# Spreading the routing scatters over the tiles and moving the rope's sum on GpSimd, in a two-layer block on one core

## The reference

```python
x = x + _L0_xattn_ref(_layernorm(x), ctx_2048, ids, ...)   # latent attention, 16 heads of 128 + rope part of 64
x = x + _L0_ffn_ref(_layernorm(x), ...)                    # 16 experts, the best 6 per token
x = x + _L1_xattn_ref(_layernorm(x), ctx_2048, mask)       # attention over 128 memory tokens
x = x + _L1_ffn_ref(_layernorm(x), ...)                    # gated MLP of 2048 plus 8 product-key experts per token
```

## Time and profile before

| | us |
|---|---|
| median of three runs | 2090.32 |
| the profiled execution | 2089.45 |
| its span | 2087.7 |
| PE busy in the span | 1836.0 (88%) |
| DVE / ACT / POOL busy | 1205.9 / 870.9 / 822.2 |
| 96 scatters, POOL line 2114 | 99.2 |

### The profile page before, as it was taken

How to read it: one execution, slowest core, us unless ns; L and a number is a source line. 1 busy time by engine, 2 the same in 40 slices (tenths; PEclk the granted TensorE clock), 3 DMA queues, 4 the chain that set the end, 5 groups by cost and what they waited for, 6 DMA issues and landing times.

```text
span 2087.7 us, 39748 instructions
## 1 busy us (share of the span) xinstructions
PE 1836.0 (88%) x13025; PEld 1086.0 (52%) x13029; DVE 1205.9 (58%) x2650; ACT 870.9 (42%) x1790; POOL 822.2 (39%) x691
## 2 busy tenths in 40 slices
PE   1586998998989489999999999997569989999998
PEld 1335666666655256666666666664444434444443
DVE  7854777777766433333333333332785677777776
ACT  3435877777666134334444344442232222212211
POOL 3102336555565533444344444442001344554542
PEclk7698999999999789999999999999689999999999
DMA  5314557776765256666676676453210345565554
GB/s 195 111 61 125 165 177 170 176 181 186 157 148 127 54 168 163 142 141 163 142 166 142 145 170 124 94 87 60 92 45 12 114 143 186 169 210 202 189 181 164
DMA packets 149136, 294.82 MB, mean 141 GB/s; under 512 B 40432, under 2 KB 77936, under 8 KB 144688
## 3 DMA queue, kind: packets, MB, share of 16 engines
q1 hardware_dynamic: 97968, 157.48, 26.5%
q0 software_dynamic: 46368, 126.29, 24.8%
q10 hardware_dynamic: 4608, 8.52, 1.3%
HBM read 426.00 MB, written 78.33 MB: 242 GB/s over the span
## 4 chain that ended last, share of the span: by engine, by line
PE 66%; issue 8%; POOL 8%; DVE 8%; ACT 5%; DMA 4%; another core or an unknown queue 1%; ACTq 0%; SPq 0%; POOLq 0%; DVEq 0%
PE bank L205 19%; PE bank L207 19%; PE bank L206 19%; POOL expert_tokens L2114 3%; PE bank L999 2%; DMA x_sum<-x,work_arena 2%; DVE work_arena L1466 2%; PE bank L1026 2%; ACT xt_arena L1246 1%; POOL work_arena L2091 1%; DVE work_arena L168 1%; DVE ln_st L155 1%; POOL xt_arena L2100 1%; DMA x<-token_rows,work_arena 1%; POOL xt_arena L2110 1%
## 5 line engine op out<-in xcount | busy, mean ns | idle before, releaser
L205 PE MATMUL bank<-work_arena,xt_arena 128*128 (+1 forms) x1285 | 417.9, 327 | 6.9 <-DVE xt_arena L174 3.3
L206 PE MATMUL bank<-work_arena,xt_arena 128*128 (+1 forms) x1285 | 417.7, 327 | 0.0
L207 PE MATMUL bank<-work_arena,xt_arena 128*128 (+1 forms) x1285 | 417.7, 327 | 0.0
L2187 POOL DMA_INDIRECT x_sum<-x,work_arena x111 | 176.3, 1589 | 400.3 <-DMA x_sum<-x,work_arena 176.7
L205 PE MATMUL bank<-work_arena 128*128 128x512 f16 (+1 forms) x680 | 260.7, 386 | 48.5 <-DVE work_arena L1466 20.0
L1940 DVE TENSOR_TENSOR xt_arena<-xt_arena,bank 128x352 f32<-128x352 f32 x111 | 57.8, 521 | 372.4 <-PE bank L207 347.7
L206 PE MATMUL bank<-work_arena 128*128 128x512 f16 (+1 forms) x680 | 261.1, 386 | 0.0
L207 PE MATMUL bank<-work_arena 128*128 128x512 f16 (+1 forms) x680 | 260.4, 385 | 0.0
L205 PE MATMUL bank<-xt_arena,work_arena 128*128 128x512 f16 (+1 forms) x560 | 212.7, 380 | 1.0 <-DVE xt_arena L174 1.0
L206 PE MATMUL bank<-xt_arena,work_arena 128*128 128x512 f16 (+1 forms) x560 | 212.3, 379 | 0.0
L207 PE MATMUL bank<-xt_arena,work_arena 128*128 128x512 f16 (+1 forms) x560 | 212.2, 379 | 0.0
(11 more groups left out here) (254 smaller groups left out, 3823.1 us busy)
## 6 DMA issues: line engine op xcount, KB each, us to landing
work_arena<-expert_w SPq DMA_DIRECT2D x111, 1408.0 KB
work_arena<-expert_w SPq DMA_DIRECT2D x111, 768.0 KB
work_arena<-in_moe_w SPq DMA_DIRECT2D x64, 352.0 KB
expert_w<-work_arena SPq DMA_DIRECT2D x86, 176.0 KB
work_arena<-in_moe_w SPq DMA_DIRECT2D x48, 256.0 KB
work_arena<-in_mlp_w SPq DMA_DIRECT2D x8, 1536.0 KB
work_arena<-in_head_w SPq DMA_DIRECT2D x16, 512.0 KB, 3.5
expert_w<-work_arena SPq DMA_DIRECT2D x64, 128.0 KB
```

What stands on the lines that cost most here:

```text
L205: pe.matmul(o, a_hi, b_hi, start=start, stop=False)
L206: pe.matmul(o, a_hi, b_lo, start=False, stop=False)
L207: return pe.matmul(o, a_lo, b_hi, start=False, stop=stop)
L2187: pool.indirect_dma_start(out=xacc[:, :], out_offset=bass.IndirectOffsetOnAxis(ap=rid[:, i:i + 1], axis=0), in_=ysb[:, b % YB, :], in_offs ...
```

## The change

Only POOL's list changes, in two places. In the second step of a tile (g = 1) the rope's sum now stands in front of the rows' low half. And the 12 scatters of a batch stand three each in steps ready+4, +5, +8 and +9 (g = 3, 0, 3, 0); for the sixth batch, in +4, +5, +6 and +7 (steps 59 to 62). In step 62 there are then six scatters, with three of the seventh batch, which stays where it was.

```diff
+            def places_of(m):
+
+                late = (4, 5, 8, 9)
+                ends = (4, 5, 6, 7)
+                return [(k, q) for q in range(INNER - 2) for k in range(4)
+                        if m == ready(q) + (late if q < INNER - 3 else ends)[k]]
+
...
                 if row_tile(m, 0) is not None:
                     row_rstd(row_tile(m, 0))
-                if row_tile(m, 1) is not None:
-                    row_low(row_tile(m, 1))
                 if t + 1 < NT:
                     if g in (1, 2):
                         rope_sum_pool(t + 1, g - 1)
                     if g in (2, 3):
                         rope_low_pool(t + 1, g - 2)
-                for k in range(3):
-                    if m - 4 - k in SCORES_AT and BATCHES[SCORES_AT[m - 4 - k]][1] == 2:
-                        place_batch(SCORES_AT[m - 4 - k], 4 * k, 4 * k + 4)
+                if row_tile(m, 1) is not None:
+                    row_low(row_tile(m, 1))
+                for k, q in places_of(m):
+                    place_batch(q, 3 * k, 3 * k + 3)
```

## The result

The changed kernel took 2081.72 us (median of six, 2077.45 to 2083.06), the one before 2093.19 (median of six, 2089.49 to 2100.2): ratio 0.9941, interval 0.9922 to 0.9961. It is 0.6% faster, and not the 1.3% forecast: 2063 was too low, and 2081.7 lies outside 2050 to 2079. Two repeats gave 0.9919 (0.9898 to 0.994) and 0.9929 (0.9909 to 0.995).

A forecast was written before the change was run, and what follows sets the result against it. PE holds 66% of the chain, so GpSimd matters only where PE waits for it. Stall -21.1, sum -7.5 and tail +1.5 gave -27.1 against 2089.45, forecast 2063 us; own range 2055 to 2072, 8 in 10 2050 to 2079.

The forecast's parts named there:

- Scatters out of g = 1: Attention tiles with four scatters in g = 1: all five PE waits at line 2096 vanish, gaining 21.1 us, bounds 10.3 to 25.1.
- The 4.0 kept for those: Fifth long tile: PE's "issue" waits at lines 858 and 859, 2.2 + 1.8 us, were expected to stay.
- Scatters in g = 3 and 0 of every tile: POOL in the attention tiles: PE's cover, 6.1 us of slack, hides these scatters; cost 0, bounds 0 and 3.8 us a step.
- The sum ahead of the rows' low half: Second step of a tile: earlier sum gains 11.1 us through ACT, DVE's delay costs 3.6; net gain 7.5.
- The sum by that rule: Sum edit with DVE's full 1.2 us block paid in each of six rank tiles: 11.1 - 7.2 = 3.9 us gained.
- The tail: Last normalizations, steps 61 and 62: six scatters make the third normalization 2.5 us late; 1.5 us lost, bounds 0 and 2.5.
- line 930 at 9.5, just under the 10 set: Sign of being wrong: PE waits at line 930, the ranks, for more than 10 us.
- the clock at 0.95 in tiles that had no stall: Sign of being wrong: a granted clock below 1.00 in tiles without a stall.
- The five long tiles near 30 us: Sign of being right: the five tiles with scatters in g = 1 fall to near 30 us, at clock 1.00.
- the half stall: Rival at line 846: half the stall stays as a new wait, -12 us, 2078; chance 0.13.
- no matter: Rival: order doesn't matter, or tail and next stage's start return the gain; within 10 us of before, 2085; chance 0.06.
- The slower one: Rival: new scatters in g = 3 delay a normalization PE waits for at line 887; +42 less 27, 2105; chance 0.05.

The follow-up runs named there:

- e6b: Changed kernel without the 72 scatters of the first six batches, run again; 2053.73 us, ratio 0.9881 to the kernel before.
- e8b: Changed kernel with two powers of one column and a drain between them on POOL in place of each of the 72 scatters; 2059.88 us, ratio 0.9861.
- e9: Changed kernel without the 72 scatters and with the rope's sum behind the rows' low half, as before; 2055.2 us, ratio 0.9891.
- e8: Changed kernel with one power of one column on POOL in place of each of the 72 scatters, nothing transferred; 2056.23 us, ratio 0.9887.
- e1: Changed kernel with the old order, rows' low half in front of the rope's sum, scatters in their new places; 2067.6 us, ratio 0.994.
- e1b: Repeat of e1 in another set, on the chip of the first; 2084.4 us, ratio 0.9957 to the kernel before.
- e10: Changed kernel without the 72 scatters, with DVE's split behind the heads' split in steps g = 1; 2047.66 us, ratio 0.9848.
- e2: Kernel before with only the new order, rope's sum in front of the rows' low half, scatters in their old places; 2089.26 us, ratio 1.0026.
- e3: Changed kernel with the old order in the six tiles with ranks and the new order elsewhere; 2066.69 us, ratio 0.9937.
- e4: Changed kernel with DVE's weight split of a tile's second step behind the heads' low half; 2065.68 us, ratio 0.9921.
- e6: Changed kernel without the 72 scatters of the first six batches; one execution, 2055.22 us, beside 2078.17 for the changed kernel.
- e4b: Repeat of e4 in another set; 2077.44 us, ratio 0.9922 to the kernel before.

## Why the prediction was wrong

Predicted -27; measured -7.8 in the profiled pair and -11.5 between the medians of six. By its own steps:

- **Scatters out of g = 1: mechanism right, size nearly.** All five waits at line 2096 are gone. The five tiles gave 18.7; the prediction had 21.1 for the stall and 5 x 0.85 for the sum, 25.4 together, so 6.7 too much. What is missing is in two tiles, 34.32 and 35.47. In the first ACT waits 3.04 us for a load at line 1293, and PE then 3.74 for ACT; in the other PE has "issue" waits, 1.9 and 1.2 the largest. The 4.0 kept for those rightly stayed. I read them as not touched by the change; they are absent without the scatters, but also in four runs with them, so what makes them stays open. Without scatters the five tiles take 148.03 (e6b), 11.9 less than here.

- **Scatters in g = 3 and 0 of every tile: the step that failed.** It compared POOL's slack, 6.1 us, with POOL's time, 1.27 a scatter. That part holds even better than I said: e8b keeps POOL as busy and loses nothing in the tiles. What the step never priced is the transfer. I dismissed the scatters' queue since nobody waits for it soon; but beside it the queue that brings the expert weights took 37% more engine time per MB, ACT's in-order list waits for those weights, and in the tile at 325.88 PE for ACT. Before, a rank tile held four scatters, in its last step; they cost it nothing (184.22, and 184.26 with none at all, e9). Now all but the first hold three in their first step too, right ahead of the ranks. They take 195.63, against 188.78 without scatters (e6b): 6.9 us that I put down to this step. The first, which has them in the last step alone, takes 31.62 in both. But no wait of PE for a load is among the 6.9. 4.3 of them are in PE's busy time, 3.5 of that in the two tiles at clock 0.95, and 2.2 are "issue" waits. e8 had such a tile at 0.95 with no transfer, and with the old order the scatters' new places cost the rank tiles 1.4 in e1 and 4.9 in e1b. So that the transfers cost is shown by e6b and e8b; by which way they reach PE in the rank tiles is not.

- **The sum ahead of the rows' low half: right where nothing blocks, wrong in rank tiles.** In the first two tiles it gave 0.90 and 1.07 where I had 0.85, and 1.11 in the seven clean ones. The ways differ from the text: of the 7.8 in these seven, 2.8 are the wait at line 871 (10.5 to 7.7), 3.8 waits at line 846 that end, and the rest is PE's busy time. In the rank tiles I had -5.1 + 3.6 = -1.5 and clean runs show +4.5. Line 930's wait grew by 5.3 (by 5.1 in the profiled pair), 1.07 in each of five rank tiles and nothing in the sixth, where I took half of a bound, 0.6, in six and had 3.6; and the gain came to only 0.8 of 5.1. Its whole price is what e10 wins by keeping the two apart, 8.8 us, more than my bound of 7.2, since the old 4.4 of waiting goes with it.

The Trainium skill (SBUF — State Buffer, Who interferes with whom) says that a DVE instruction with two SBUF inputs and a GpSimd instruction that reads SBUF exclude each other for the whole instruction. The trace agrees: 0.88 became 1.95, and the sum ended 1.20 after the split had started. Where the split has 512 columns, 0.68 became 1.75, the same 1.07 more. The sum by that rule, 3.9 for this edit, is near the clean 3.3; I had set it aside for 7.5. Term by term it is further off, 11.1 for 8.6 and 7.2 for 5.3, so part of its nearness is luck.

- **The tail: right in size, half by luck.** +1.8 for +1.5. The third normalization comes 30.45 after scores(60), for 29.59: 0.9 late, not 2.5. The first of the three comes 17.05 after scores(60), for 20.02: 3.0 earlier and not 1.27, since step 60 has one scatter less too. What the other 0.9 of the 1.8 is, no run shows. In the first set this stretch took 76.53 with the old places (e2) and 79.17 and 79.14 with the new ones (e3, e4): 2.6 more. POOL's list shows the six in a row, two of them here:

```profile
666.85 1.05 POOL L2100 TENSOR_TENSOR xt_arena<-xt_arena,work_arena 128x512 f32<-128x512 f32 x1
668.07 1.00 POOL L2114 DMA_INDIRECT expert_tokens<-work_arena  x1 [0.17 <-issue]
...
674.48 0.97 POOL L2114 DMA_INDIRECT expert_tokens<-work_arena  x1 [0.30 <-issue]
675.45 1.07 POOL L2100 TENSOR_TENSOR xt_arena<-xt_arena,work_arena 128x512 f32<-128x512 f32 x1
```

Against the forecast of the thirteen tiles, -28.6, the measured -9.2 leaves 19.3: 6.7 in the five tiles, 12.9 in the rank tiles (6.0 the order, 6.9 the scatters), less 0.3 in the first two. So the step on the scatters in g = 3 and 0 accounts for up to 13.6 of it and the order for 6.0. Outside the tiles +2.2 came before scores(8), in a part that the change doesn't touch, and +1.8 in the tail; from line 999 on, at 732.90 for 738.17, another 2.6 went away, which I can't assign. Of the signs named in advance, two warned of it: line 930 at 9.5, just under the 10 set, and the clock at 0.95 in tiles that had no stall. Of the signs of being right two came true: line 2096 is gone from PE's waits, and the 2.5 us at line 1224 from ACT's. The five long tiles near 30 us did not. The rivals: none is it. By number 2081.7 lies between the half stall (2078) and "no matter" (2085), but no half of the stall stayed. The slower one put its price on line 887, which shows no wait at all.

Open: why the price of the scatters differs between chips and sets. Without those 72 the thirteen tiles take 396.07, 396.03 and 396.04 on three chips (e6, e6b, and e8b with POOL busy); with them the changed kernel takes 414.75, 415.32 and 421.32, and the kernel before 423.99 and 441.00. Nor did a run tell whether it is the number of the scatters' packets (32 each: 1728 for the 54 scatters between 325 and 600 us), their size (0.03 MB in all), or their random places that slows the others.

## What to carry to other kernels

A DMA that is moved to where nobody waits for it can still have a price: ask which loads run beside it and who waits for those in order. Before sizing a small reordering, take the noisy neighbour out of both versions; in clean tiles differences of 0.3 us could be read here, while the thirteen tiles of one program differed by up to 17 between sets. And a gain must be followed to the next fixed loop: what ACT won before PE's transposes could never pass them.

## What the hardware showed that I had not expected

- An indirect scatter of 128 x 4 bytes holds POOL 1.27 us. As much time of POOL cost nothing in the tiles (e8b), and the scatters' packets take 0.4% of the DMA engines' time, yet the loads and stores beside them took 37% more engine time per MB.
- PE's "issue" waits at lines 856 to 860 are 6.1 us in the changed kernel, 9.2 in e1b and none in e1, which is the same program, nor in the six runs without scatters. They make most of the 10 us between e1 and e1b, and of the 11 between e4 and e4b. The page lists an instruction queue among the DMA queues; that the engines' own instructions come late through it is my guess, not shown.
- A stall's length doesn't decide the clock alone: e6b waits 2.31 us at line 930 in a tile at clock 1.00, the changed kernel 2.31 and 2.56 in tiles at 0.95. e8 has e6b's tile with the same wait at 0.95, and takes 33.87 for 32.19.
- A power of one column took POOL 0.53 to 0.55 us in e8. At line 2106 of the changed kernel it takes 0.57 to 0.59 behind scores(60), but 0.95 to 1.15 in the tiles; why, no run shows.
- DVE's subtraction beside POOL's sum takes 1.07 us longer, whether it has 512 columns (0.68 to 1.75) or 704 (0.88 to 1.95).
